# The first gate product of a pass: the input's low half moved to its end, and the wait with it

## The chip, the cores and the metric

The kernel runs on one core of a Trainium2 chip. The metric is the device time of one launch in microseconds, taken as the median of several runs. A second, profiled execution gives the trace from which all rows below are taken.

The engines are named as in the profile: PE is TensorE (matmuls), PEld its weight loads, DVE is VectorE, ACT is ScalarE, POOL is GpSimd, SP is SyncE, which issues the DMAs.

## The reference, cut to what matters

The input is 2 sequences of 1024 tokens with 128 channels. Four blocks follow each other, each with a residual sum and a layer norm without gain ahead of it:

```
x = x + attn_a(layernorm(x))     # a scan over time with a fixed decay per channel
x = x + ffn(layernorm(x))        # 8 experts, all of them for every token
x = x + attn_b(layernorm(x))     # a recurrence with an 8 x 8 state per head
x = x + ffn(layernorm(x))        # the same 8 experts with the same weights
```

The change is in the feed-forward part, which for every expert e is

```
g = einsum('bsh,ehf->ebsf', x, w_gate)
u = einsum('bsh,ehf->ebsf', x, w_up)
h = silu(g) * u
expert_out = einsum('ebsf,efh->ebsh', h, w_down)
out = einsum('ebsh,bse->bsh', expert_out, cw)      # cw: routing weights
```

with 8 experts and 512 hidden channels each.

## The kernel before

**Tiling.** The 2048 tokens are 16 tiles of 128. The feed-forward part goes over them in passes of 4 tiles (512 tokens): passes 0 to 3 are the first feed-forward block, passes 4 to 7 the second. A pass has 32 slots (8 experts by 4 chunks of 128 hidden channels), so there are 256 slots, numbered through: slot 0 opens pass 0, slot 128 pass 4, slot 192 pass 6. A slot g is: the gate product on PE (`gate g`), silu on ACT (`silu g`, line L1049), the up product on PE (`up g`), their product on DVE (`hidden g`, L1662, tile sh_buf), and two halves of the down product on PE (`down g 0`, `down g 1`, w_down by sh_buf). After four slots an expert's sum is scaled on ACT (`weigh`, L1163) and added to x on POOL (`add`, L946).

**Split products.** The normed input of a pass is kept as a high half `z_hi` (a rounded copy, made by ACT at L1029 and counted by the semaphore ln_out) and a low half `z_lo` (what is left, made by DVE at L1673 and counted by z_low). The weights are split alike, into w_hi and w_lo. A gate or up product is three matmuls into one PSUM bank (L1222, through the helper mm): w_hi by z_lo, w_lo by z_hi, w_hi by z_hi. The first gate of a pass waits for z_low ahead of all three.

**What comes ahead of a pass.** For pass q: statistics of x (DVE L1548, L1551; POOL L875, L877), centring and scaling (DVE L1560, L1565, tile normed), four transposes on PE (`ffn_z q`, L1236), the high half on ACT, the low half on DVE (`ffn_low q`), and a full copy zf for the router (`ffn_copy q`, ACT L1036; `route q` on PE).

**What sets the order.** Each engine runs a fixed list. A planner at the head of the file (class Plan, in plain Python, before the kernel is built) makes the lists: every operation has an engine, a duration and a list of what it follows. At each step an engine takes, of the operations that could start within NEAR of the earliest, the one with the highest rank plus a hand-set lead per group (LEAD). The planner also hands out the 8 PSUM banks. So a change in what an operation follows can move operations of every engine. What an engine waits for when it runs is written separately, in the functions that issue the instructions (gate_part, split_product and so on).

**Names used later.** Of attn_a: `mix`, `kv`, `scan`, `r`, `inner` (DVE L1578 to L1608, PE), `mid_T` (PE L1266), `mid_out`, `mid_add`. `restart 0` clears the state tiles for attn_b with four memsets on DVE (L1841 to L1846). Of attn_b's read-out, for pass 3 of it: `y0 3 i` is a product and a reduction on DVE (L1882, L1884), `through` a product on POOL (L936), `y1` a reduction on DVE (L1890); `back_z`, `back_hidden`, `back_out` are on PE, `back_add` (L1916) on DVE.

Of the kernel before, what the change touches and what calls it, by code (L numbers as in the profile page):

```python
# [68 lines left out]
PE_SUM = 1.75  # L69
PE_SUMS = dict(T2=[0, 0, 1, 1, 1, 1, 0, 1, 1, 1, 1, 0, 1, 1, 1, 1], W2=[1, 1, 1, 1, 1, 0, 1, 1, 1, 1, 1, 1, 1, 1, 1, 1])  # L70
SWITCH = 0.08
TABLE_LOAD, HOP, START = 1.28, 0.07, 5.0
CHUNK_TIME = 2.40
WEIGHT = dict(pe=1.60, act=1.10, dve=1.31, pool=1.10, sp=1.02)
# [42 lines left out]
def experts():  # L117

    out = []
    for g in range(SLOTS):  # L120
        q, c = divmod(g, CHUNKS)
        e, f = divmod(g, FC)
        after = (on("pe", "gate", g - 1),) if g else ()
        if c == 0:
            after += (on("dve", "ffn_low", q),)
        if q == 0 and f == 0:
            after += (on("pool", "split", 2 * e), on("pool", "split", 2 * e + 1))
        if g > AHEAD:
            after += (on("dve", "hidden", g - 1 - AHEAD),)
        out.append(pe(("gate", g), 0.7, *after, takes=((("gate", g), on("act", "silu", g)),)))  # L130
        after = (on("act", "silu", g - 1),) if g else ()
        if g >= 2:
            after += (on("dve", "hidden", g - 2),)
        out.append(act(("silu", g), 0.6, on("pe", "gate", g), *after, table="silu"))
        after = (on("pe", "up", g - 1),) if g else ()
        out.append(pe(("up", g), 0.7, on("pe", "gate", g), *after, takes=((("up", g), on("dve", "hidden", g)),)))
        after = (on("dve", "hidden", g - 1),) if g else ()
        if g >= 4:
            after += (on("pe", "down", g - 4, 1),)
        if g == 3:  # L140
            after += (on("pool", "split", 2),)
        out.append(dve(("hidden", g), 0.69, on("act", "silu", g), on("pe", "up", g), *after))
        after = (on("pe", "down", g - 1, 1),) if g else ()
        out.append(pe(("down", g, 0), 0.41, on("dve", "hidden", g), *after, takes=((("y", e), on("act", "weigh", e, 1) if e < PASSES * E - 1 else on("dve", "add_last")),) if f == 0 else ()))
        out.append(pe(("down", g, 1), 0.41, on("pe", "down", g, 0)))
    for e in range(PASSES * E - 1):
        after = (on("pool", "add", e - 1),) if e else ()
        if e % E == 0:
            after += (on("dve", "combine", e // E),)
        out.append(act(("weigh", e, 0), 0.73, on("pe", "down", FC * e + FC - 1, 1), *after))  # L150
        out.append(act(("weigh", e, 1), 0.73, on("act", "weigh", e, 0)))
        out.append(pool(("add", e), 1.26, on("act", "weigh", e, 1), port=True))
    out.append(dve(("add_last",), 1.1, on("pe", "down", SLOTS - 1, 1), on("pool", "add", PASSES * E - 2)))
    return out
# [197 lines left out]
class Plan:  # L352
# [65 lines left out]
    def start(self, k):  # L418
# [15 lines left out]
            begin = max([begin] + [t for t, _ in free[:len(o.takes)]])  # L434
        return begin

    def banks(self):
        out = []
        for name in BANKS:
            freer = self.bank_free[name]  # L440
            if freer is None:
                out.append((0.0, name))
            elif freer in self.end:
                out.append((self.end[freer] + HOP, name))
        return sorted(out)
# [18 lines left out]
    def pick(self, engine):  # L464
        found = []
        for k in self.ready[engine]:
            begin = self.start(k)
            if begin is not None:
                o = self.ops[k]
                if engine == "act" and o.table and o.table != self.table:  # L470
                    found.append((begin + NEAR, begin, k))
                else:
                    found.append((begin, begin, k))
        if not found:
            return None
        near = min(found)[0] + NEAR
        return max((self.ops[k].rank + self.lead(self.ops[k]), -begin, k) for soon, begin, k in found if soon <= near)

    def run(self):
        for k, n in list(self.waiting.items()):  # L480
# [67 lines left out]
def build(nc, a, out):  # L548
    ctx = ExitStack()
    with ctx:  # L550
# [669 lines left out]
        def _(pe):  # L1220
# [99 lines left out]
                if half == 1:  # L1320
                    ins.then_inc(S["y_full" if f == FC - 1 else "d_done"], 1)

            def split_product(bank, lo, hi, q):

                mm(bank, hi, z_lo[:, q % 2, :], stop=False)
                mm(bank, lo, z_hi[:, q % 2, :], start=False, stop=False)
                return mm(bank, hi, z_hi[:, q % 2, :], start=False)

            def sum_rows(bank, product):

# [81 lines left out]
            def gate_part(g):  # L1412
                q, c = divmod(g, CHUNKS)
                e, f = divmod(c, FC)
                cols_f = slice(f * P, (f + 1) * P)
                if c == 0:
                    pe.wait_ge(S["z_low"], q + 1)
                if q == 0 and f == 0:
                    pe.wait_ge(S["w_split"], 2 * e + 2)
                name = BANK["gate", g]  # L1420
                take(name)
                split_product(bank_named[name][:], w_lo[:, e, 0, cols_f], w_hi[:, e, 0, cols_f], q).then_inc(S["g_full"], 1)
                free[name] = (S["silu_done"], g + 1)

            def up_part(g):
# [621 lines left out]
```

## Time and profile before

| | us |
|---|---|
| median of 3 runs | 926.3 (925.91 to 928.23) |
| the profiled execution | 925.21 |
| its span, first to last instruction | 923.2 |
| PE busy in the span | 850.2 (92%) |
| DVE busy | 562.0 (61%) |
| ACT busy | 401.0 (43%) |
| POOL busy | 409.2 (44%) |

The profiled execution is 2.0 us longer than its span and 1.1 us shorter than the median. A busy time is a sum over the span; whether an engine sets the pace of a stretch is read from the stretch, since the program goes through stages in which PE never stops and stages in which PE waits for DVE and POOL.

### The profile page before, as it was taken

The page shows a single profiled execution, that of the slowest core. Times are in us where ns is not written, and L with a number is a line of the kernel's source. Part 1 is how long each engine was busy: PE and PEld are TensorE (multiplying, and loading weights), DVE is VectorE, ACT ScalarE, POOL GpSimd, SP SyncE. Part 2 cuts the span into 40 slices and gives each one's busy share as a digit, 9 for nine tenths or more (in the row PEclk, how much of TensorE's full clock was granted, in tenths as well). Part 3 has the DMA queues.
Part 4 walks back from the last instruction along what each step waited for, and adds up shares of the span by engine and source line. Part 5 has one row for each costly group of instructions (what it writes and reads, how often), then busy time and mean ns, then how long its engine had stood idle before and what let it go on. Part 6 is the DMA issues. An engine that isn't in the chain of part 4 may idle for free.

```text
span 923.2 us, 13835 instructions
## 1 busy us (share of the span) xinstructions
PE 850.2 (92%) x5170; PEld 717.0 (78%) x5170; DVE 562.0 (61%) x927; ACT 401.0 (43%) x874; POOL 409.2 (44%) x287
## 2 busy tenths in 40 slices
PE   3399999989898999999999799799999799999998
PEld 1287987779767888998786487787999678888887
DVE  6669544298819994226698886888112959543222
ACT  5145337653374343334837536134334254544432
POOL 3435311048704876564262674578652624220211
PEclk9699999999999999999999899799999999999999
DMA  9400000011101100012210111111002211000000
GB/s 282 98 1 2 1 1 1 1 46 46 47 1 46 47 24 24 1 47 92 92 46 1 46 47 46 47 46 47 12 1 92 92 46 58 1 2 1 12 1 12
DMA packets 20710, 35.87 MB, mean 39 GB/s; under 512 B 3062, under 2 KB 9636, under 8 KB 20644
## 3 DMA queue, kind: packets, MB, share of 16 engines
q1 hardware_dynamic: 20644, 35.00, 11.5%
q8 instruction: 41, 0.67, 0.3%
q14 instruction: 25, 0.20, 0.1%
HBM read 21.36 MB, written 13.63 MB: 38 GB/s over the span
## 4 chain that ended last, share of the span: by engine, by line
PE 54%; DVE 9%; issue 2%; ACT 1%; POOL 0%; DVEq 0%; ACTq 0%; POOLq 0%
PE bank L1222 53%; DVE states L1882 1%; DVE sh_buf L1662 1%; DVE w_a L1884 1%; DVE backs L1865 1%; DVE scr L1890 1%; DVE state L1786 0%; PE bank L1236 0%; DVE work L1761 0%; DVE state L1794 0%; ACT sh_buf L1049 0%; ACT w_sb L1137 0%; ACT backs L1121 0%; POOL work L888 0%; DVE stats L1548 0%
## 5 line engine op out<-in xcount | busy, mean ns | idle before, releaser
L1662 DVE TENSOR_TENSOR sh_buf<-sh_buf,bank 128x512 f32<-128x512 f32 x256 | 172.8, 684 | 264.2 <-PE bank L1222 225.6
L1222 PEld LDWEIGHTS bank<-w_down,sh_buf 128*128 128x128 f32 x2048 | 274.9, 193 | 47.9 <-DVE sh_buf L1662 24.7
L1222 PE MATMUL bank<-w_down,sh_buf 128*128 128x128 f32 x2048 | 294.8, 281 | 16.2 <-DVE sh_buf L1662 16.2
L1049 ACT ACTIVATE sh_buf<-bank 128x512 f32<-128x512 f32 x256 | 152.3, 598 | 304.7 <-PE bank L1222 227.9
L1222 PE MATMUL bank<-z_lo,w_hi 128*128 128x512 f32 x512 | 234.5, 458 | 0.9 <-DVE z_lo L1673 0.9
L1222 PE MATMUL bank<-z_hi,w_lo 128*128 128x512 f32 x512 | 204.0, 398 | 0.0
L1222 PE MATMUL bank<-z_hi,w_hi 128*128 128x512 f32 x512 | 203.3, 397 | 0.0
L946 POOL TENSOR_TENSOR x<-x,y_weighted 128x512 f32<-128x512 f32 x63 | 88.5, 1405 | 224.7 <-ACT y_weighted L1163 224.7
L1222 PEld LDWEIGHTS bank<-z_hi,w_hi 128*128 128x128 f32 x512 | 96.9, 189 | 23.4
L1222 PEld LDWEIGHTS bank<-z_lo,w_hi 128*128 128x128 f32 x512 | 98.6, 193 | 14.5 <-issue 3.9
L1222 PEld LDWEIGHTS bank<-z_hi,w_lo 128*128 128x128 f32 x512 | 98.6, 193 | 9.0 <-issue 1.2
L926 POOL TENSOR_TENSOR backs<-backs,head_mask 128x512 f32<-128x512 f32 x64 | 70.2, 1101 | 50.5 <-PE bank L1222 45.8
L1163 ACT ACTIVATE y_weighted<-bank,cw 128x128 f32<-128x128 f32 x252 | 72.9, 369 | 24.1 <-PE bank L1222 22.2
L1222 PEld LDWEIGHTS bank<-states,backs 128*128 128x128 f32 x512 | 72.0, 191 | 7.8 <-issue 1.9
L936 POOL TENSOR_TENSOR backs<-backs,w_a 128x1024 f32<-128x1024 f32 x16 | 41.9, 2627 | 62.1 <-DVE w_a L1884 41.1
L1222 PE MATMUL bank<-states,backs 128*128 128x8 f32 x512 | 65.9, 237 | 0.1
L1222 PE MATMUL bank<-work,ident 128*128 128x128 f32 x384 | 51.3, 292 | 9.7 <-DVE work L1761 8.2
L1222 PEld LDWEIGHTS bank<-work,ident 128*128 128x128 f32 x384 | 49.0, 206 | 14.3 <-DVE work L1761 9.6
L1130 ACT ACTIVATE states<-bank 128x16 f32<-128x16 f32 x126 | 23.0, 183 | 70.0 <-PE bank L1222 69.9
L888 POOL TENSOR_TENSOR work<-quad,rkv 128x1024 f32<-128x1024 f32 x16 | 32.3, 2016 | 42.3 <-DVE quad L1737 31.8
L914 POOL TENSOR_TENSOR readout<-state,rkv 128x1024 f32<-128x1024 f32 x16 | 40.5, 2529 | 23.5 <-DVE state L1797 15.1
L906 POOL TENSOR_TENSOR state<-state,work 128x1024 f32<-128x1024 f32 x16 | 43.6, 2724 | 0.9
(206 smaller groups left out, 927.8 us busy)
## 6 DMA issues: line engine op xcount, KB each, us to landing
trans_spill<-state SPq DMA_DIRECT2D x16, 512.0 KB, 2.6
backs<-trans_spill SPq DMA_DIRECT2D x16, 512.0 KB, 3.5
backs<-keep_spill SPq DMA_DIRECT2D x4, 1024.0 KB, 5.5
x<-in_x SPq DMA_DIRECT2D x4, 256.0 KB, 5.2
backs<-in_w_gate SPq DMA_DIRECT2D x4, 256.0 KB, 6.0
backs<-in_w_up SPq DMA_DIRECT2D x4, 256.0 KB, 6.2
keep_spill<-rkv SPq DMA_DIRECT2D x4, 256.0 KB, 2.6
keep_spill<-low SPq DMA_DIRECT2D x4, 256.0 KB, 2.9
```

Of the source, the lines that this page charges most:

```text
L888: pool.tensor_tensor(outer.rearrange("p (h i k) -> p h i k", h=H, i=N), vs[:, i, :].rearrange("p (h i) -> p h i", h=H).unsqueeze(3).broadc ...
L906: pool.tensor_tensor(trans, trans, prod_t, ALU.subtract).then_inc(S["trans_rdy"], 1)
L914: pool.tensor_tensor(readout[:].rearrange("p (h i k) -> p h i k", h=H, i=N), locst.rearrange("p (h i k) -> p h i k", h=H, i=N), over_i(rec ...
L926: pool.tensor_tensor(blocks_d[:, p % RING].rearrange("p c b (h i) -> p (c b) h i", h=H), src.unsqueeze(2).broadcast_to((P, PIECE * B, H, N ...
L936: pool.tensor_tensor(t_ring[t % 2].rearrange("p (h i j) -> p h i j", h=H, i=N), t_ring[t % 2].rearrange("p (h i j) -> p h i j", h=H, i=N), ...
L946: pool.tensor_tensor(flat(x[:, G * j:G * j + G, :]), flat(x[:, G * j:G * j + G, :]), y_weighted[:], ALU.add).then_inc(S["x_added"], 1)
L1049: act.activation(s_buf[:, m % 2, :], bank_of("gate", m)[:], ACT.Silu).then_inc(S["silu_done"], 1)
L1130: act.activation(dst, bank_of("links", u)[:, first:first + B * N].rearrange("p (b k) -> p b k", b=B), ACT.Copy).then_inc(S["link_rdy"], 1)
L1163: ins = act.activation(y_weighted[:, i * P:(i + 1) * P], bank_of("y", eg)[:, i * P:(i + 1) * P], ACT.Identity, scale=cw[:, q % 2, i, e:e + 1])
L1222: return pe.matmul(dst, lhs, rhs, start=start, stop=stop, **kw)
L1662: dve.tensor_tensor(h_buf[:, m % 4, :], s_buf[:, m % 2, :], bank_of("up", m)[:], ALU.mult).then_inc(S["h_done"], 1)
L1865: dve.tensor_tensor(rows_hi(fin_w), rows_hi(locst), dend, ALU.mult).then_inc(S["fin_rdy"], 1)
```

## The change

Three things are changed in the code.

1. In every gate and up product the three matmuls stand in the order w_lo by z_hi, w_hi by z_hi, w_hi by z_lo.
2. The first gate of a pass waits for ln_out (the high half is there) ahead of its first matmul, and for z_low ahead of its third.
3. In the planner, the first gate of a pass follows the high half (`ffn_z q` on ACT) instead of the low half, and the first up product of a pass follows the low half (`ffn_low q`). A term `stick` is added to the priority; its constant STICK is 0.0. LEAD is untouched.

```diff
         if c == 0:
-            after += (on("dve", "ffn_low", q),)
+            after += (on("act", "ffn_z", q),)
...
         after = (on("pe", "up", g - 1),) if g else ()
+        if c == 0:
+            after += (on("dve", "ffn_low", q),)
         out.append(pe(("up", g), 0.7, on("pe", "gate", g), *after, takes=((("up", g), on("dve", "hidden", g)),)))
...
+    def stick(self, k):
+
+        if k[0] != "pe" or not ORDER["pe"]:
+            return 0.0
+        last, kind = ORDER["pe"][-1][0], k[1][0]
+        return STICK if (kind in ("gate", "up") and last in ("gate", "up")) or (kind == last == "down") else 0.0
...
-            def split_product(bank, lo, hi, q):
-
-                mm(bank, hi, z_lo[:, q % 2, :], stop=False)
-                mm(bank, lo, z_hi[:, q % 2, :], start=False, stop=False)
-                return mm(bank, hi, z_hi[:, q % 2, :], start=False)
+            def split_product(bank, lo, hi, q, first=False):
+
+                mm(bank, lo, z_hi[:, q % 2, :], stop=False)
+                mm(bank, hi, z_hi[:, q % 2, :], start=False, stop=False)
+                if first:
+                    pe.wait_ge(S["z_low"], q + 1)
+                return mm(bank, hi, z_lo[:, q % 2, :], start=False)
...
                 if c == 0:
-                    pe.wait_ge(S["z_low"], q + 1)
+                    pe.wait_ge(S["ln_out"], LN["ffn", q] + 1)
...
-                split_product(bank_named[name][:], w_lo[:, e, 0, cols_f], w_hi[:, e, 0, cols_f], q).then_inc(S["g_full"], 1)
+                split_product(bank_named[name][:], w_lo[:, e, 0, cols_f], w_hi[:, e, 0, cols_f], q, c == 0).then_inc(S["g_full"], 1)
```

The planner's lists differ in 40 places on PE, 23 on ACT, 30 on DVE and 4 on POOL, nearly all of them in slots 2 to 17, around slot 35, and in slots 185 to 214. The order at the first gate of passes 0 and 4 is the same as before, the new order inside the product aside. In the changed kernel all line numbers are larger by 10 on PE and by 12 on DVE.

**PE at the head of pass 6.** The row of transposes is `ffn_z 6`. Before, it is followed by down 189, up 191, down 190, then gate 192 (the first gate of pass 6), down 191, gate 193.

```order
L1236 MATMUL bank<-ident,normed 128x128 x4
L1222 MATMUL bank<-w_down,sh_buf 128x128 x4
L1222 MATMUL bank<-z_lo,w_hi 128x512
L1222 MATMUL bank<-z_hi,w_lo 128x512
L1222 MATMUL bank<-z_hi,w_hi 128x512
L1222 MATMUL bank<-w_down,sh_buf 128x128 x4
L1222 MATMUL bank<-z_lo,w_hi 128x512
L1222 MATMUL bank<-z_hi,w_lo 128x512
L1222 MATMUL bank<-z_hi,w_hi 128x512
L1222 MATMUL bank<-w_down,sh_buf 128x128 x4
```

Now up 191 stands ahead of the transposes, and they are followed by down 190 and 191, gate 192, gate 193. The wait for z_low stands ahead of the first z_lo row.

```order
L1232 MATMUL bank<-z_hi,w_lo 128x512
L1232 MATMUL bank<-z_hi,w_hi 128x512
L1232 MATMUL bank<-z_lo,w_hi 128x512
L1246 MATMUL bank<-ident,normed 128x128 x4
L1232 MATMUL bank<-w_down,sh_buf 128x128 x8
L1232 MATMUL bank<-z_hi,w_lo 128x512
L1232 MATMUL bank<-z_hi,w_hi 128x512
L1232 MATMUL bank<-z_lo,w_hi 128x512
L1232 MATMUL bank<-z_hi,w_lo 128x512
```

Down 191 has moved from behind gate 192 to ahead of it, and up 191 from behind the transposes to ahead of them.

**DVE at the same place.** Before, the scaling of the norm is followed by `y0 3 0` (two rows) and then by the low half z_lo; hidden 191 comes behind z_lo.

```order
L1565 TENSOR_TENSOR normed<-normed,rstd 128x512
L1882 TENSOR_TENSOR states<-w_sb,backs 128x1024
L1884 TENSOR_REDUCE w_a<-states 128x128
L1673 TENSOR_TENSOR z_lo<-bank,z_hi 128x512
L1662 TENSOR_TENSOR sh_buf<-sh_buf,bank 128x512
L1882 TENSOR_TENSOR states<-w_sb,backs 128x1024
```

Now hidden 191 stands ahead of `y0 3 0`.

```order
L1577 TENSOR_TENSOR normed<-normed,rstd 128x512
L1674 TENSOR_TENSOR sh_buf<-sh_buf,bank 128x512
L1894 TENSOR_TENSOR states<-w_sb,backs 128x1024
L1896 TENSOR_REDUCE w_a<-states 128x128
L1685 TENSOR_TENSOR z_lo<-bank,z_hi 128x512
L1674 TENSOR_TENSOR sh_buf<-sh_buf,bank 128x512
```

One more operation (hidden 191, which needs up 191 from PE) stands between the norm and the low half.

**PE at slots 15 to 16.** The rows are up 15, gate 16, the first half of down 14, and the transposes `mid_T 2`. Before:

```order
L1222 MATMUL bank<-z_hi,w_hi 128x512
L1222 MATMUL bank<-z_lo,w_hi 128x512
L1222 MATMUL bank<-z_hi,w_lo 128x512
L1222 MATMUL bank<-z_hi,w_hi 128x512
L1222 MATMUL bank<-w_down,sh_buf 128x128 x2
L1266 MATMUL bank<-ident,quad 128x128 x4
```

Now:

```order
L1232 MATMUL bank<-z_lo,w_hi 128x512
L1232 MATMUL bank<-w_down,sh_buf 128x128 x2
L1232 MATMUL bank<-z_hi,w_lo 128x512
L1232 MATMUL bank<-z_hi,w_hi 128x512
L1232 MATMUL bank<-z_lo,w_hi 128x512
L1276 MATMUL bank<-ident,quad 128x128 x4
```

The half of down 14 has moved from behind gate 16 to ahead of it. On DVE, in the same slots, the four memsets of `restart 0` have moved from behind hidden 13 to ahead of hidden 10.

## Rows read from the trace of the kernel before

**Rows 1.** The page, section 1: busy time of each engine.

```profile
PE 850.2 (92%) x5170; PEld 717.0 (78%) x5170; DVE 562.0 (61%) x927; ACT 401.0 (43%) x874; POOL 409.2 (44%) x287
```

**Rows 2.** Busy time by stretch: stretch, its length, then each engine, granted clock, DMA.

```profile
62.00:91.00 29.00, 29.00 (x165) 23.11 (x163) 24.51 (x53) 15.80 (x33) 13.30 (x10) 1.00 0.01 1
493.00:517.00 24.00, 17.87 (x61) 10.41 (x62) 22.63 (x48) 15.22 (x25) 10.05 (x8) 0.91 0.08 23
743.00:820.00 77.00, 76.82 (x450) 63.81 (x450) 49.66 (x92) 37.91 (x73) 21.97 (x17) 1.00 0.10 32
```

**Rows 3.** The page, section 5: the z_lo matmuls; last, the idle time ahead of them.

```profile
L1222 PE MATMUL bank<-z_lo,w_hi 128*128 128x512 f32 x512 | 234.5, 458 | 0.9 <-DVE z_lo L1673 0.9
```

**Rows 4.** Timeline of PE behind gate 192: start, duration, operation.

```profile
763.40 1.05 PE L1222 MATMUL bank<-w_down,sh_buf 128*128 128x128 f32 x8
764.20 0.48 PE L1222 MATMUL bank<-z_lo,w_hi 128*128 128x512 f32 x1
...
764.98 0.40 PE L1222 MATMUL bank<-z_lo,w_hi 128*128 128x512 f32 x1
...
765.68 0.39 PE L1222 MATMUL bank<-z_lo,w_hi 128*128 128x512 f32 x1
```

**Rows 5.** Timeline at gate 0.

```profile
44.67 0.68 DVE L1673 TENSOR_TENSOR z_lo<-bank,z_hi 128x512 fp32r<-128x512 f32 x1
45.57 0.77 PE L1222 MATMUL bank<-z_lo,w_hi 128*128 128x512 f32 x1
```

**Rows 6.** Timeline at gate 128, and PE's next long wait.

```profile
492.12 0.58 ACT L1029 ACTIVATE z_hi<-bank 128x512 fp32r<-128x512 f32 x1
492.73 0.69 DVE L1673 TENSOR_TENSOR z_lo<-bank,z_hi 128x512 fp32r<-128x512 f32 x1 [1.82 <-ACT z_hi L1029]
493.44 0.61 ACT L1144 ACTIVATE states<-ones 32x512 f32<-32x512 f32 x1
493.48 0.50 PE L1222 MATMUL bank<-z_lo,w_hi 128*128 128x512 f32 x1 [0.88 <-DVE z_lo L1673]
...
494.28 1.99 PE L1222 MATMUL bank<-w_a,b_ow 128*128 128x512 f32 x4
...
516.81 1.97 PE L1222 MATMUL bank<-backs,b_w 128*64 128x512 f32 x2 [4.27 <-DVE sh_buf L1662]
```

**Rows 7.** Timeline of PE around gate 192.

```profile
759.48 0.66 PE L1236 MATMUL bank<-ident,normed 128*128 128x128 f32 x4
759.97 1.06 PE L1222 MATMUL bank<-w_down,sh_buf 128*128 128x128 f32 x8
...
761.33 0.40 PE L1222 MATMUL bank<-z_hi,w_hi 128*128 128x512 f32 x1
...
762.59 0.51 PE L1222 MATMUL bank<-z_lo,w_hi 128*128 128x512 f32 x1
```

**Rows 8.** Timeline of DVE around gate 192.

```profile
759.34 1.22 DVE L1882 TENSOR_TENSOR states<-w_sb,backs 128x1024 f32<-128x1024 f32 x1
...
761.85 0.69 DVE L1673 TENSOR_TENSOR z_lo<-bank,z_hi 128x512 fp32r<-128x512 f32 x1
762.46 0.68 DVE L1662 TENSOR_TENSOR sh_buf<-sh_buf,bank 128x512 f32<-128x512 f32 x1
763.05 2.35 DVE L1882 TENSOR_TENSOR states<-w_sb,backs 128x1024 f32<-128x1024 f32 x1
```

**Rows 9.** Timeline of DVE and PE at slots 13 to 16.

```profile
88.68 1.56 DVE L1604 SCALAR_TENSOR_TENSOR work<-rkv,cols,low 128x512 f32<-128x512 f32 x1
...
91.00 1.28 DVE L1662 TENSOR_TENSOR sh_buf<-sh_buf,bank 128x512 f32<-128x512 f32 x2
...
91.74 0.71 PE L1222 MATMUL bank<-w_down,sh_buf 128*128 128x128 f32 x4 [0.72 <-DVE sh_buf L1662]
```

**Rows 10.** The page, section 5: weight loads of one matrix used 8 times running.

```profile
L1222 PEld LDWEIGHTS bank<-work,ident 128*128 128x128 f32 x384 | 49.0, 206 | 14.3 <-DVE work L1761 9.6
L1222 PE MATMUL bank<-work,ident 128*128 128x128 f32 x384 | 51.3, 292 | 9.7 <-DVE work L1761 8.2
```

More of the change, by code:

```diff
@@ L71 @@
 SWITCH = 0.08
+STICK = 0.0
 TABLE_LOAD, HOP, START = 1.28, 0.07, 5.0
@@ L476, in pick @@
         near = min(found)[0] + NEAR
-        return max((self.ops[k].rank + self.lead(self.ops[k]), -begin, k) for soon, begin, k in found if soon <= near)
+        return max((self.ops[k].rank + self.lead(self.ops[k]) + self.stick(k), -begin, k) for soon, begin, k in found if soon <= near)
     def run(self):
```

## The prediction, made before the changed kernel ran

> **What bounds the kernel now.** I read the page first: PE is busy for 850 of 923 us [rows 1]. Then the busy time by stretch, because a mean over the span says nothing about a place. From 743 to 820 us, where pass 6 opens, PE is busy for 76.8 of 77 us: there every microsecond that PE waits is added to the end. From 62 to 91 us PE never stops while DVE fills 24.5 of 29 us, so both are close to the bound. From 493 to 517 us, where pass 4 opens, DVE is busy for 22.6 of 24 us and PE only for 17.9: there DVE sets the pace [rows 2]. Last, how much PE waited for the low half in the whole span: the group of the z_lo matmuls shows 0.9 us, once [rows 3]. That is the most that the late wait can give back directly, and the question is where that 0.9 us lies.
>
> **The new order inside a product costs nothing.** The same 1536 matmuls run. A product directly behind another takes 0.70 us (764.98 to 765.68), so 0.23 per matmul; one behind a down product takes 0.78 (764.20 to 764.98) [rows 4]. The longer first matmul is thus a matter of place, not of z_lo, and will pass to the w_lo row. A down product of two halves and the product behind it take 763.40 to 764.98, 1.58 us, so the two halves add 0.88 to the product's 0.70 wherever they stand [rows 4]. PE work that is only put in another order keeps its sum.
>
> What speaks for a gain is that two matmuls with the same w_hi now follow each other. The trace has such runs: eight matmuls with the identity as weights, 384 in all, and they have 384 weight loads [rows 10]. The load is made each time, beside the matmul ahead of it, and I count nothing. If it fell away and the 27 ns by which the 233 ns of a matmul exceed a load's 206 ns [rows 4, 10] went with it, 512 products would save 14 us. It is the last of the rivals. The Trainium skill ("TensorE: Matmul & The Clock Gate", step-by-step part of the matmul) says that weights can be loaded once and then used by many matmuls; the rows of the identity do not show it.
>
> **Pass 0.** z_lo ends at 45.35, gate 0 starts at 45.57, 0.22 later, while the hop from DVE to PE elsewhere is about 0.05 (762.54 to 762.59) [rows 5, 7, 8]. PE was occupied with transposes and did not wait. Gain 0.
>
> **Pass 4.** Here lies the 0.88 us. The high half is there at 492.70, the low half at 493.42, gate 128 starts at 493.48 [rows 6]. Now it can start at about 492.75, and its third matmul, due at 493.3, waits to 493.47, so the gate ends some 0.5 us sooner. But the next instruction, back_hidden 1 (494.28 before), needs ACT's states tile, which ends at 494.05: PE comes 0.2 us ahead. And PE's next long wait, 4.27 us up to 516.81, is for a hidden product on DVE [rows 6], which stands in a queue that has been full since 492.73 and that neither the gate nor its order enters. So the 0.2 us makes that wait longer and the end no sooner. Gain 0; the bounds are 0 and 0.9.
>
> **Pass 6 loses.** The planner now lets gate 192 follow the high half alone and hangs the low half on up 192. But the engine does what the code says: the wait stands inside gate 192, ahead of its third matmul, and gate 193, which the planner put ahead of up 192 as cover, is queued behind that wait. Arrival on PE: in the old order gate 192 would have started 0.23 + 0.80 us behind the last matmul of up 191 (761.33), at 762.36; it started at 762.59 when z_lo was there, 0.23 late [rows 7, 4]. In the new order down 191 comes first, 0.88 more: gate 192 starts at 763.24 and its third matmul is due at 0.78 - 0.23 = 0.55 later, 763.79. The low half on DVE: hidden 191 now stands ahead of `y0 3 0`. It needs up 191, whose last matmul ended at 761.73; the transposes now come behind it, which puts it 0.49 earlier (759.48 to 759.97), at 761.24 [rows 7]. Hidden 191 starts at 761.29; 0.59 later (762.46 to 763.05) `y0 3 0` starts; 2.51 later (759.34 to 761.85) z_lo starts, and takes 0.69 [rows 8]. z_lo is there at 765.08, PE sees it at 765.13. PE waits 765.13 - 763.79 = 1.34 us, where it waited 0.23 before: **+1.1 us**. All that PE has behind it waits too (gates 193 and 194, ups 192 and 193, route 6), and PE is the bound. The bounds: 0, if DVE comes to `y0 3 0` early enough; 2.2, if its product takes the 2.35 us that one of them took beside POOL's, instead of 1.22 [rows 8].
>
> The other moves from slot 185 to 214 (back_hidden, back_out, back_z 3, ffn_z 7 each one or two tasks later) find their inputs ready by my walk through both queues; `y0 3 1` comes about 4.5 us later, since hidden 192 now stands ahead of it and needs up 192.
>
> **Slots 2 to 17.** The half of down 14 needs hidden 14 and waited for it: DVE 91.00 plus 0.69, PE at 91.74 after 0.72 us of idle time, with gate 16 already done [rows 9]. DVE's queue up to hidden 14 holds the same work as before (the four memsets of restart 0 only come earlier), and it is nearly without a gap, so hidden 14 stays at about 91.6. But gate 16 (0.70 us) now stands behind the half of down 14, and comes that much later. From this I take 0.2 for gaps that DVE loses: **+0.5 us**. PE waits in two places for it, before down 12 (hidden 12 is pushed back by the memsets) and before down 14. Until 147 us every wait of DVE is for PE, so the delay is handed on. Bounds: 0.8, gate 16 whole; -0.4, if L1604, which took 1.56 us at 88.68, falls beside no POOL work any more and saves 0.8.
>
> **Slot 35 and around 300 us:** a front norm 0.4 us later and two tasks swapped, all with a margin behind them. 0, with 0.3 either way.
>
> **The sum.** The profiled execution took 925.2; 925.2 + 1.1 + 0.5 = 926.8. It lies 1.1 below the median of the runs, so against the median the forecast is 926.3 + 1.6 = **927.9 us**. A measurement of this kernel can tell about 0.3% (2.8 us) from no change, so this is "the same" with a loss inside.
>
> **Rivals.**
> - **Nothing moves.** `y0 3 0` starts before PE needs the low half, and the waits of the early slots only change places: 926.3, within 925.3 to 927.0. For it: the sums at both places are differences of tenths between queues. Against it: in pass 6 a hidden product that needs PE is put ahead of z_lo, and 2.5 us of DVE work lies between.
> - **Slower: DVE becomes the bound of pass 6.** PE's slot is about 2.3 us; DVE's share of it is 0.69 plus a `y0` of 2.5 in every other slot. If the later `y0` meet POOL's products, each takes 1.13 more (2.35 against 1.22 [rows 8]). Three of them make 3.4 us, of which the 1.4 us or so that hidden products run ahead of their down products swallow a part: 2.0 more, on top of 1.6, 929.9. It decides from the second slow one on. Against it: at 743 to 820 us DVE is busy for only 49.7 of 77 us [rows 2].
> - **Faster: pass 4 hands its gain on.** From 493 to 517 us the granted clock is 0.91 on average [rows 2], so part of it ran at 1.2 GHz. If an idle time less kept PE at 2.4 GHz for the W2 sum that follows 516.81, DVE's chain behind it would gain some 2 to 4 us: 923. Against it: the 4.27 us wait ahead of it stays and even grows.
> - **Weights are not loaded twice:** 926.3 - 14 = 912, against 384 loads for 384 matmuls [rows 10].
>
> **How the numbers follow.** Forecast (927.0 to 929.1) 0.50; nothing moves 0.28; slower by DVE or by a stretch at the low clock behind the new wait 0.14; faster by pass 4 0.07; loads 0.01. Forecast and "nothing moves" lie within 0.3% (923.5 to 929.1). So faster 0.08, same 0.78, slower 0.14. The range reaches from 924.4, which takes in the lower bounds of slots 2 to 17 and of pass 4 and the spread of the runs, to 930.2, which takes in the DVE case: 924.4 to 930.2.
>
> **What would show it.** In the changed profile: the first w_lo row of gate 128 at about 0.7 us after the high half starts to be read, and the long wait before front_hidden 3 still over 4 us; the z_lo matmuls with an idle time of about 1.3 us by z_lo at gate 192 and some 0.2 at gate 128; `y0` rows between hidden 191 and z_lo on DVE; an idle time of about 0.9 before the half of down 14, with gate 16 behind it; the w_lo matmuls now with the larger mean, near 458 ns, and z_lo's near 397. The sum is wrong if gate 192's third matmul does not wait, if the early waits are below 0.5 us, or if the stretches at the lower clock change in number or length: one of them moved is worth as much as all my terms together.

## The result, and the profile after

The changed kernel took **928.27 us** (median of 12 runs, 926.5 to 929.85) against 926.96 us (12 runs, 924.91 to 928.51) of the kernel before beside it: ratio **1.0023**, 95% interval 1.0013 to 1.0032. By this ratio it is 2.1 us more: inside the 0.3% that the prediction counts as the same, and with an interval above 1. The ratio is not the quotient of the two medians, which lie only 1.31 us apart; the size of the loss is known no better than that from the times. In a second series it was 1.0021 (1.0007 to 1.0035). The profiled execution took 928.20 us, its span 926.3 us at a mean clock of 0.967; before, 925.21 and 923.2 us at 0.972. In the second series its span was 924.2 at 0.973. The two traces of one kernel thus differ by 2.1 us, as much as the change costs, and the difference of two whole spans proves nothing here. What can be compared are stretches between two fixed tasks, which agree between traces to some hundredths of a microsecond where the granted clock is alike. One profiled execution, that of the experiment code_only, took 1687 us and is left out everywhere.

The busy time by stretch after the change answers to [rows 2] (stretch, its length, then each engine, granted clock, DMA):

```profile
62.00:91.00 29.00, 28.11 (x161) 22.57 (x161) 24.97 (x53) 15.82 (x33) 11.91 (x9) 1.00 0.00 1
493.00:517.00 24.00, 16.97 (x64) 9.14 (x62) 22.10 (x47) 15.86 (x26) 9.25 (x8) 0.94 0.07 23
743.00:820.00 77.00, 75.31 (x438) 61.71 (x437) 47.19 (x86) 37.04 (x72) 21.72 (x15) 1.00 0.10 31
```

PE never stopped in the first stretch and was busy for 76.8 us in the last; now it stops for 0.9 and for 1.7 us. The page's groups of the products, with the idle time ahead of them, answer to [rows 3]:

```profile
L1232 PE MATMUL bank<-z_hi,w_lo 128*128 128x512 f32 x512 | 234.8, 459 | 0.2 <-ACT z_hi L1039 0.2
L1232 PE MATMUL bank<-z_lo,w_hi 128*128 128x512 f32 x512 | 204.2, 399 | 1.1 <-DVE z_lo L1685 1.1
L1232 PE MATMUL bank<-z_hi,w_hi 128*128 128x512 f32 x512 | 204.9, 400 | 0.0
```

The mean of 459 ns has passed from z_lo to w_lo, and the idle time by z_lo is 1.1 us, where it was 0.9: the change was to take a wait for z_lo away and has more of it. It only lies elsewhere. PE at gate 192 (start, duration, operation, idle time before):

```profile
762.82 0.66 PE L1246 MATMUL bank<-ident,normed 128*128 128x128 f32 x4
763.31 1.95 PE L1232 MATMUL bank<-w_down,sh_buf 128*128 128x128 f32 x16
765.01 0.48 PE L1232 MATMUL bank<-z_hi,w_lo 128*128 128x512 f32 x1
765.33 0.39 PE L1232 MATMUL bank<-z_hi,w_hi 128*128 128x512 f32 x1
766.86 0.50 PE L1232 MATMUL bank<-z_lo,w_hi 128*128 128x512 f32 x1 [1.14 <-DVE z_lo L1685]
767.21 0.39 PE L1232 MATMUL bank<-z_hi,w_lo 128*128 128x512 f32 x1
```

And DVE ahead of it:

```profile
757.02 0.69 DVE L1928 TENSOR_TENSOR x<-x,bank 128x512 f32<-128x512 f32 x1 [2.83 <-PE bank L1232]
...
761.41 0.69 DVE L1674 TENSOR_TENSOR sh_buf<-sh_buf,bank 128x512 f32<-128x512 f32 x1 [1.06 <-ACT sh_buf L1059]
762.02 0.74 DVE L1577 TENSOR_TENSOR normed<-normed,rstd 128x512 f32<-128x512 f32 x1
763.01 0.69 DVE L1674 TENSOR_TENSOR sh_buf<-sh_buf,bank 128x512 f32<-128x512 f32 x1 [0.25 <-issue]
763.61 1.22 DVE L1894 TENSOR_TENSOR states<-w_sb,backs 128x1024 f32<-128x1024 f32 x1
764.87 1.22 DVE L1896 TENSOR_REDUCE w_a<-states 128x128 f32<-128x1024 f32 x1
766.12 0.69 DVE L1685 TENSOR_TENSOR z_lo<-bank,z_hi 128x512 fp32r<-128x512 f32 x1
768.86 0.69 DVE L1674 TENSOR_TENSOR sh_buf<-sh_buf,bank 128x512 f32<-128x512 f32 x1 [2.05 <-PE bank L1232]
```

Hidden 191 (763.01), the two instructions of `y0 3 0`, then z_lo: DVE reaches it at 766.12 and the third matmul waits. The rows of pass 4 answer to [rows 6]:

```profile
493.54 0.50 PE L1232 MATMUL bank<-z_hi,w_lo 128*128 128x512 f32 x1 [0.15 <-ACT z_hi L1039]
493.88 0.40 PE L1232 MATMUL bank<-z_hi,w_hi 128*128 128x512 f32 x1
494.26 0.50 PE L1232 MATMUL bank<-z_lo,w_hi 128*128 128x512 f32 x1
494.60 1.99 PE L1232 MATMUL bank<-w_a,b_ow 128*128 128x512 f32 x4
...
517.63 1.97 PE L1232 MATMUL bank<-backs,b_w 128*64 128x512 f32 x2 [6.08 <-DVE sh_buf L1674]
```

Here the change does what it says: the wait at the gate is 0.15 us instead of 0.88. And PE's next long wait is 6.08 us instead of 4.27, so none of it arrives.

**Stretches between tasks.** All traces of this study in one table: microseconds from the start of the first task's first matmul to that of the second's. The kernels are explained with the experiments below. "Lists" says whose order of the work they run; a number is that of the tasks put elsewhere in it.

```
                          lists      gate 8-  gate 40- gate 127-  gate 133- gate 187- gate 195- gate 205-
                                     mid_T 2  gate 48  fr_hid 3 5 gate 170  gate 195  gate 205  gate 220
before                    before      27.52    30.38    36.10     144.16     24.63     22.94     41.39
code_again                before      27.55    30.38    36.11     144.15     24.53     22.94     43.00
extra                     before      27.54    30.38    36.09     144.11     25.53     22.93     41.39
out_late                  before+1    27.54    30.37    36.10     144.14     26.19     22.94     41.39
after                     after       27.77    30.54    36.12     144.79     25.84     22.94     41.61
after_again               after       27.77    30.51    36.10     144.04     25.85     22.94     41.60
plan_only                 after       27.75    30.52    36.09     144.82     26.32     22.94     41.61
low_first                 after+1     27.76    30.51    36.10     144.69     24.44     24.19     41.61
low_y_late                after+2     27.78    30.56    36.11     144.03     24.43     24.18     42.97
out_early                 after+4     27.77    30.54    36.10     144.71     25.12     22.94     41.61
early_back                after+2     29.31    30.53    36.09     144.77     27.40     22.94     41.60
```

From gate 220 to the last down product every trace has 84.99 us. The loss of the changed kernel is in four places: +1.21 us where pass 6 opens, +0.25 in slots 8 to 17, +0.22 between gates 205 and 220, +0.16 between gates 40 and 48: 1.84 us in all, between the 1.3 us of the medians and the 2.1 us of the ratio.

The two small ones are waits too short for the profile to name. Between gates 205 and 220 it is the transposes of pass 7 in the changed kernel:

```profile
822.39 0.69 DVE L1577 TENSOR_TENSOR normed<-normed,rstd 128x512 f32<-128x512 f32 x1 [0.65 <-POOL rstd L887]
822.55 0.60 PE L1232 MATMUL bank<-w_down,sh_buf 128*128 128x128 f32 x4
823.14 0.66 PE L1246 MATMUL bank<-ident,normed 128*128 128x128 f32 x4
```

The norm is ready at 823.08 and the transposes start at 823.14, 0.59 us behind the half of a down product; before, the same step took 0.45 us. Their norm is late because `back_add 3`, which it follows, starts 23.77 us behind gate 205 instead of 21.92: `back_out 3` has come later on PE. Between gates 40 and 48 the first products that read the front's hidden layer (`tokA 0 0`) start at 164.73, 0.05 us after ACT ended that layer (164.68); before, ACT was 0.45 us ahead (163.73 and 164.18).

### The profile page after: what moved, and what is told of

Its sections match the earlier page's. It is cut to its first block, busy times and chain, and to the rows that moved or that the text cites. A ratio compares the mean times of both kernels' runs of the same rounds, so it can differ in the third digit from the quotient of the medians.

```text
span 926.3 us, 13835 instructions
## 1 busy us (share of the span) xinstructions
PE 851.7 (92%) x5170; PEld 716.9 (77%) x5170; DVE 559.4 (60%) x927; ACT 401.9 (43%) x874; POOL 408.3 (44%) x287
## 4 chain that ended last, share of the span: by engine, by line
PE 50%; DVE 10%; issue 3%; POOL 2%; ACT 1%; DVEq 0%; POOLq 0%; ACTq 0%
PE bank L1232 50%; DVE states L1894 1%; DVE sh_buf L1674 1%; DVE w_a L1896 1%; DVE backs L1877 1%; POOL state L916 1%; DVE scr L1902 0%; DVE state L1798 0%; POOL work L906 0%; POOL work L898 0%; DVE work L1773 0%; DVE state L1809 0%; DVE state L1806 0%; DVE quad L1764 0%; POOL readout L924 0%
## 5 line engine op out<-in xcount | busy, mean ns | idle before, releaser
L1232 PEld LDWEIGHTS bank<-w_down,sh_buf 128*128 128x128 f32 x2048 | 274.3, 192 | 49.3 <-DVE sh_buf L1674 24.4
L1232 PE MATMUL bank<-z_hi,w_lo 128*128 128x512 f32 x512 | 234.8, 459 | 0.2 <-ACT z_hi L1039 0.2
L1232 PE MATMUL bank<-z_lo,w_hi 128*128 128x512 f32 x512 | 204.2, 399 | 1.1 <-DVE z_lo L1685 1.1
L1232 PEld LDWEIGHTS bank<-z_hi,w_hi 128*128 128x128 f32 x512 | 98.8, 193 | 9.1 <-issue 1.2
```

Source lines behind the costliest of these rows:

```text
L1232: return pe.matmul(dst, lhs, rhs, start=start, stop=stop, **kw)
```

## Experiments

Each was timed in five rounds beside the kernel before; ratios are to it, with 95% intervals. Nothing is left out of the computation in any of them. In the diffs `move(engine, task, target)` takes a task out of the finished list of an engine and puts it ahead of the target, with `False` behind it.

### code_only and code_again: the new engine code under the old lists

Against the changed kernel, in the planner's rules for gate and up:

```
         if c == 0:
-            after += (on("act", "ffn_z", q),)
+            after += (on("dve", "ffn_low", q),)
...
-        if c == 0:
-            after += (on("dve", "ffn_low", q),)
```

> The new order inside the products and the late wait for z_low, with the planner's rules of before, so every engine's list of operations is that of before. Theory (the loss is in the planner's lists): no loss. Gate 128 starts 0.7 us sooner and the end does not move; at gate 192 the 0.23 us of waiting goes. From gate 187 to gate 195 the trace shows 24.4 us (24.63 before). Time: that of before, -0.2 to 0 us. Rival (the new product order or the wait inside the gate costs by itself): 1 us or more slower than before. Second rival (pass 4's 0.88 us is worth something): 0.5 to 0.9 us faster.

> The changed engine code (the low half's product last, with its own wait) under the lists of the kernel before; the same text as code_only, for a profile that can be read. Theory (the code is free, its lists are what costs): within 0.1% of before; in the profile gate 8 to mid_T 2 takes 27.5 us as before (27.76 with the new lists), gate 187 to gate 195 takes 24.63 or, with the 0.23 us of waiting at gate 192 gone, 24.4 (25.8 with the new lists), gate 195 to 205 22.94, gate 205 to 220 41.39; gate 128 starts 0.7 us earlier and the wait ahead of front_hidden 3 5 is near 5 us instead of 4.27, so gate 127 to front_hidden 3 5 stays at 36.1. Rival (the late wait itself or the longer first matmul costs): the 1.2 us of pass 6 are there with the old lists too, 0.13% slower.

Measured: code_only 925.51 us, ratio 0.9990 (0.9976 to 1.0005). The same text ran again as code_again: 926.52 us, 1.0003 (0.9991 to 1.0015), span 924.2. The page of code_again:

```profile
L1230 PE MATMUL bank<-z_hi,w_lo 128*128 128x512 f32 x512 | 234.4, 458 | 0.2 <-ACT z_hi L1037 0.2
L1230 PE MATMUL bank<-z_hi,w_hi 128*128 128x512 f32 x512 | 203.9, 398 | 0.0
L1230 PE MATMUL bank<-z_lo,w_hi 128*128 128x512 f32 x512 | 203.6, 398 | 0.0
```

PE never waits for z_lo any more: both of the waits that there were, 0.88 at gate 128 and 0.23 at gate 192, are gone. Pass 6 gains 0.10 (24.53 against 24.63), pass 4 nothing. So the code itself costs nothing, and of the 0.9 us that the wait for z_lo showed, the end gets some 0.1. The expected 24.4 was 24.53.

### plan_only: the new lists under the old engine code

Against the kernel before, in the same rules:

```
         if c == 0:
-            after += (on("dve", "ffn_low", q),)
+            after += (on("act", "ffn_z", q),)
...
+        if c == 0:
+            after += (on("dve", "ffn_low", q),)
```

> The new lists of the planner with the engine code of before: z_lo first in every product, the wait ahead of all three matmuls. Theory: the loss stays and grows by the two matmuls that may no longer run ahead of the wait at gate 192, 0.55 us: PE waits about 1.8 us there, gate 187 to gate 195 takes 26.4 us (25.84 in the changed kernel, 24.63 before). Time: 0.5 us above the changed kernel, 2 to 3 above before. Rival (the cost is in the code): the time of before.

Measured: 929.50 us, 1.0030 (1.0015 to 1.0045). Gate 187 to gate 195 takes 26.32 us, and the three smaller losses have their full size (27.75, 30.52 and 41.61 us in the table). All of the loss is here, without the change's code, and the code takes back 0.5 of it (25.84): with the wait ahead of the whole product, its first two matmuls stand behind z_lo too.

### low_first: the low half ahead of `y0 3 0`

```
+move("dve", ("ffn_low", 6), ("y0", 3, 0))
```

> The changed kernel with one operation moved on DVE: the low half of pass 6 stands ahead of y0 3 0 instead of behind it. Theory (the 2.5 us of y0 ahead of z_lo make PE wait): the low half is there before PE needs it, the wait of 1.14 us at gate 192 is gone, gate 187 to gate 195 takes 24.6 us instead of 25.84, and the time is 1.2 us below the changed kernel. Rival (PE would have lost the same time behind it, on hidden products or banks): the wait goes and others take its place, time as the changed kernel.

Measured: 929.43 us, 1.0023 (1.0010 to 1.0035): nothing gained. At gate 192 the expected 1.2 us are there: gate 187 to gate 195 fell from 25.84 to 24.44 us. But from gate 195 to gate 205 it takes 24.19 us instead of 22.94. The one wait that PE's timeline shows from 762 to 795 us:

```profile
773.60 1.16 PE L1240 MATMUL bank<-w_down,sh_buf 128*128 128x128 f32 x8 [0.90 <-DVE sh_buf L1682]
```

It is down 193, which needs hidden 193, and DVE ahead of that:

```profile
768.31 0.69 DVE L1682 TENSOR_TENSOR sh_buf<-sh_buf,bank 128x512 f32<-128x512 f32 x1 [0.36 <-ACT sh_buf L1067]
768.92 2.65 DVE L1902 TENSOR_TENSOR states<-w_sb,backs 128x1024 f32<-128x1024 f32 x1
771.60 1.22 DVE L1904 TENSOR_REDUCE w_a<-states 128x128 f32<-128x1024 f32 x1
772.85 0.69 DVE L1682 TENSOR_TENSOR sh_buf<-sh_buf,bank 128x512 f32<-128x512 f32 x1
```

Hidden 192, `y0 3 1`, hidden 193. The first instruction of `y0 3 1` takes 2.65 us instead of 1.22, and a POOL product runs beside it:

```profile
768.09 2.39 POOL L954 TENSOR_TENSOR backs<-backs,w_a 128x1024 f32<-128x1024 f32 x1 [5.14 <-issue]
```

In the changed kernel `y0 3 1` starts at 769.46, behind the POOL product, and takes 1.22. Here, what is taken from one wait is paid in the next.

### low_y_late: `y0 3 1` out of the way as well

```
+move("dve", ("ffn_low", 6), ("y0", 3, 0))
+move("dve", ("y0", 3, 1), ("hidden", 193), False)
```

> low_first (the low half of pass 6 ahead of y0 3 0) with y0 3 1 moved behind hidden 193 as well. In low_first the 1.2 us gained at gate 192 went again between gates 195 and 205 (24.19 us instead of 22.94), where the half of down 193 waited for a hidden product behind y0 3 1. Theory (that place in DVE's queue is what costs): gate 195 to 205 falls to 22.9 to 23.3 us, gate 187 to 195 stays at 24.4, and the time is 0.8 to 1.2 us below the changed kernel's, 0.10 to 0.14% over before. Rival (DVE has no room there, so any order of it hands the 1.2 us to another wait): gate 187 to 205 stays at 48.6 and the time at 0.2% over before.

Measured: 927.91 us, 1.0008 (0.9996 to 1.0019). The theory's place is clean, down 193 no longer waits, yet gate 195 to gate 205 takes 24.18 us as in low_first. The longest wait stands three slots further on, at down 196, and shorter ones that no row names stand around it:

```profile
777.73 1.16 PE L1241 MATMUL bank<-w_down,sh_buf 128*128 128x128 f32 x8 [0.56 <-DVE sh_buf L1683]
```

The rival holds for the stretch: wherever the two `y0` stand, about 1.2 us reach PE by gate 205 (gate 187 to 205: 48.78 in the changed kernel, 48.63 and 48.61 in these two, 47.57 before). That the median is nevertheless below low_first's does not come from this stretch. The timed runs differ in clock: the mean granted clock of its 12 runs is 0.9715, that of low_first's 12 is 0.9659. That this is the whole difference is not shown.

### out_late: one move in the kernel before

If neither of two other orders of DVE's queue in pass 6 helps, its work may arrive too late as a whole. PE's timeline ahead of pass 6 shows how it could. `back_out 2`, the 3.3 us of W2 products that feed the residual, stands ahead of gate 189 in the old list; in the new one it stands behind gate 189, up 188 and half of down 187, 1.84 us of PE work later. DVE's `back_add 2` (757.02 in the changed kernel, released by PE), the norm of pass 6, z and both `y0` hang on it.

code_only with one line more:

```
+move("pe", ("back_out", 2), ("down", 187, 0), False)
```

> code_only (the changed engine code under the lists of before) with one task moved: back_out 2 on PE, the 3.3 us that feed the residual of pass 6, stands behind gate 189, up 188 and the first half of down 187, as it does in the changed kernel, instead of ahead of gate 189. Theory (what costs in pass 6 is that its chain, back_add, norm, z, low half, starts 1.84 us of PE work later, and DVE's two y0 with it): gate 187 to gate 195 grows from 24.5 us to 25.6 to 26.0, z_lo's matmul at gate 192 waits some 1 to 1.5 us for DVE, the time is 0.1 to 0.15% over before. Rival (the places of hidden 191 and y0 3 0 on DVE are the cause, as forecast): gate 187 to 195 stays within 0.3 of 24.5 and the time within 0.03% of code_only.

Measured: 928.51 us, 1.0019 (1.0006 to 1.0033). This single move in the old lists costs more than the new lists do: gate 187 to gate 195 is 26.19 us, against 24.53 in code_again without it and 25.84 in the changed kernel: 1.66 us, somewhat more than expected. The waits are not at z_lo, though:

```profile
761.46 1.16 PE L1238 MATMUL bank<-w_down,sh_buf 128*128 128x128 f32 x8 [0.68 <-DVE sh_buf L1680]
763.88 0.66 PE L1252 MATMUL bank<-ident,normed 128*128 128x128 f32 x4 [0.55 <-DVE normed L1583]
```

PE waits for a hidden product behind `back_add 2` and for the norm itself, since this list has the transposes early. The new lists put them behind up 191 and so turned these two waits into one, at z_lo.

### out_early: the head of the chain put back in the changed kernel

```
+move("pe", ("back_out", 2), ("gate", 189))
+move("pe", ("up", 190), ("down", 188, 0))
+move("dve", ("hidden", 188), ("ffn_centre", 6), False)
+move("dve", ("y0", 3, 0), ("hidden", 191))
```

> The changed kernel with the head of pass 6's chain put back: on PE back_out 2 ahead of gate 189 and up 190 ahead of down 188, on DVE hidden 188 behind ffn_centre 6 and y0 3 0 ahead of hidden 191; gate 192, the transposes and the low half stay where the change put them. Theory (the chain's start is the cause): norm 6 and y0 3 0 start 1.1 to 1.9 us earlier, z_lo is there before gate 192's third matmul is due, gate 187 to 195 falls from 25.8 to 24.4 to 24.9, gate 195 to 205 stays below 23.3, the time is about 0.1% below the changed kernel's, so 0.10 to 0.13% over before. Rival (DVE hands the 1.2 us on whatever stands first, as in low_first and low_y_late): gate 187 to 205 stays at 48.6 to 48.8.

Measured: 927.29 us, 1.0015 (1.0002 to 1.0027). Gate 187 to gate 195 falls to 25.12 us and gate 195 to gate 205 stays at 22.94: gate 187 to 205 is 48.07, so 0.71 of the 1.21 us are back and are **not** paid later. It missed the expected 24.4 to 24.9 by one wait, which `y0 3 0` ahead of hidden 191 makes:

```profile
764.48 1.16 PE L1243 MATMUL bank<-w_down,sh_buf 128*128 128x128 f32 x8 [0.54 <-DVE sh_buf L1685]
```

z_lo is there in time; no row of gate 192 waits. In the ratios the step from 1.0023 to 1.0015 lies inside the intervals; the stretches carry the verdict.

One thing this experiment does not separate. It puts back the start of the chain and, with `y0 3 0` ahead of hidden 191, also the order that the prediction named as the cause. The trace of the changed kernel says that the early start alone would not have brought z_lo sooner: there DVE stood idle for 0.25 us ahead of hidden 191 (763.01), which needs up 191 from PE. The old lists with hidden 191 alone ahead of `y0 3 0` were not run.

### extra: what 0.9 us on PE are worth at the two gates

The kernel before, ahead of the first gate's product:

```
+                if g in (4 * CHUNKS, 6 * CHUNKS):
+                for _ in range(4):
+                    mm(bank_named[name][:], w_hi[:, e, 0, cols_f], z_hi[:, q % 2, :])
```

> The kernel before, with four more matmuls of w_hi and z_hi (0.93 us) in front of the product at gate 128 and at gate 192; their result is overwritten. It measures where 0.9 us on PE count. Theory (pass 4 is paced by DVE, pass 6 by PE): of gate 128's 0.93 us nothing arrives, gate 127 to front_hidden 3 5 stays at 36.1 and the wait of 4.27 ahead of it falls to about 3.3; at gate 192 all 0.93 arrives, gate 187 to 195 grows from 24.63 to 25.5 and the end by 0.9 us: 0.10% slower. Rival (PE counts alike at both places): both grow by 0.93, 0.20% slower.

Measured in the trace: gate 127 to front_hidden 3 5 is 36.09 us, as in every other kernel. Of pass 4's 0.93 us nothing arrives. Gate 187 to gate 195 is 25.53, 0.90 more, and the last down product starts 0.9 later relative to gate 187: of pass 6's all arrives. The theory's sizes are right. Its wait of "about 3.3" was not: it is 4.87 us, since this trace has no low clock at 503 us (granted clock 0.99 from 493 to 517, against 0.91), so PE arrived earlier in spite of the added work, and still gained nothing. The four matmuls themselves:

```profile
762.91 1.20 PE L1222 MATMUL bank<-z_hi,w_hi 128*128 128x512 f32 x4
763.95 0.39 PE L1222 MATMUL bank<-z_lo,w_hi 128*128 128x512 f32 x1
```

The time does not show it: 926.09 us, 0.9995 (0.9985 to 1.0005), where the trace would give 1.0010. The clocks of the timed runs say where to look. The mean granted clock of its 12 runs is 0.9725, that of the 29 runs of before beside it 0.9699, and among those 29 the spans are 923.5 us at a clock of 0.972 and 925.9 us at 0.968. Where the two kernels have runs at the same clock, extra's span (one run at each) is longer than the mean of before's each time: 926.7 against 925.5 us at 0.970, 924.9 against 924.3 at 0.971, 924.7 against 923.5 at 0.972. Why extra ran at the higher clock more often is open. Two medians of this kernel can't be told apart to a microsecond unless their clocks are alike.

### early_back: the early slots

```
+move("dve", ("restart", 0), ("inner", 3))
+move("pe", ("gate", 16), ("down", 14, 0))
```

> The changed kernel with the two moves of the early slots undone: restart 0 back behind its place before inner 3 on DVE, gate 16 back ahead of the half of down 14 on PE. Theory: gate 8 to mid_T 2 falls from 27.76 to 27.5 us, gate 187 to 195 stays at 25.8, and the time is 0.25 us (0.03%) below the changed kernel's, so 0.17 to 0.2% over before. Rival (more of the loss comes from the early slots than the interval shows): 0.1% or less over before.

Measured: 931.52 us, 1.0048 (1.0032 to 1.0064); both theories missed. Gate 8 to mid_T 2 takes 29.31 us, 1.5 more than in the changed kernel. The half of down 14 now waits for hidden 14 like this:

```profile
94.07 0.71 PE L1241 MATMUL bank<-w_down,sh_buf 128*128 128x128 f32 x4 [1.76 <-DVE sh_buf L1683]
```

In the old lists the memsets follow a z_lo at 85.53; in the new ones this z_lo is at 88.63, three microseconds later, and the memsets put behind it push hidden 14. It is no undoing of one part: two tasks of a list were put back into a list in which their neighbours had moved. Of the rest, 1.56 us lie where pass 6 opens (27.40 us against 25.84): this trace has a granted clock of 0.50 from 759.5 to 762.9 us, inside that stretch. The size of the early slots comes from code_again instead, 27.55 against 27.77.

### after_again: the changed kernel once more

> The changed kernel once more, as a control on the same chip and for a second trace. Theory: 1.2 to 1.7 us slower than before; gate 187 to gate 195 takes 25.8 us again and gate 8 to the transposes mid_T 2 27.8 us again (27.52 before). The stretch at 1.2 GHz at 640 us, which the first trace of it shows and before's does not, may be absent: then the profiled span is about 0.8 us shorter.

Measured: 928.61 us, 1.0021 (1.0007 to 1.0035). Its stretches in the table repeat those of the first trace to 0.03 us, except one: gate 133 to gate 170 takes 144.04 instead of 144.79. The first row is that of the first trace, the second that of the second at the same time (columns as in the busy time by stretch; the last but two is the granted clock):

```profile
640.40:643.80 3.40, 3.40 (x9) 2.67 (x9) 3.33 (x4) 3.40 (x5) 1.81 (x2) 0.50 0.02 5
```

```profile
640.40:643.80 3.40, 2.87 (x14) 1.78 (x12) 2.97 (x4) 2.85 (x5) 3.11 (x3) 1.00 0.06 22
```

A granted clock of 0.50 (1.2 GHz) for 3.4 us costs 0.75 us there. It is in five of the seven traces with the new lists or lists near them, and in none of the four with the old ones; eleven traces are too few to say whether the lists have a part in it.

## Why the prediction was right, and where it was not

The forecast was 927.9 us and "the same, with a loss inside"; it came to 928.27. That the number is so near is in part luck. The forecast stood on a median of 926.3 us from three runs, and 12 runs of the same kernel gave 926.96: the step was forecast as 1.6 us and is 1.3 by the medians, 2.1 by the ratio and 1.84 by the stretches. And inside the 1.84 one term came to half its size, while 0.38 us came from places that were put at nothing. Step by step:

- **New order inside a product: 0.** Right. code_again holds it, and the means passed from row to row as said (459 and 399 ns against 458 and 397).
- **Loads: no gain.** Right. The page of after has 512 loads for each of the three kinds of product, and z_hi,w_hi and z_lo,w_hi follow each other with the same weights:

```profile
L1232 PEld LDWEIGHTS bank<-z_lo,w_hi 128*128 128x128 f32 x512 | 97.5, 190 | 25.4 <-DVE z_lo L1685 2.0
L1232 PEld LDWEIGHTS bank<-z_hi,w_hi 128*128 128x128 f32 x512 | 98.8, 193 | 9.1 <-issue 1.2
```

- **Pass 4: 0.** Right, with its reason. The freed 0.7 us made the wait for DVE longer; even 0.93 us of added work came to nothing.
- **Pass 6: +1.1.** It measured +1.21. Shifted by the 1.69 us by which this trace is late at gate 188, hidden 191 ran at 761.32 (forecast 761.29), z_lo started at 764.43 (764.39), the third matmul started 1.30 us after it was due (1.34). The missing 0.1 is the matmul behind a wait: from it to the next are 0.35 us, not 0.23.
- **But its cause went only half the way.** The prediction named hidden 191 ahead of `y0 3 0` as what makes z_lo late, and for the wait at gate 192 that is what the trace shows. low_first puts z_lo ahead of `y0 3 0`, and the loss comes back 8 us later, so there is more to it. What the prediction said of the other moves (back_hidden, back_out and others, each one or two tasks later) is that they "find their inputs ready". That is true and is the step that misled: back_out's inputs are ready, but whoever needs its output, DVE's whole chain of pass 6, gets it 1.84 us of PE work later. I asked of each moved task whether it must wait, and not who waits for it. Out_late shows that this move alone costs 1.66 us; taking it back together with three others, `y0 3 0` among them, brings 0.71. So two things act here, the late chain and the order on DVE, and the loss of 1.21 us is less than the late chain cost alone; only the late chain was run by itself. The sum was right all the same because hidden 191 had to wait for up 191 in any case, which the prediction had in its walk.
- **The DVE rival** (`y0` meeting POOL, 2.0 more) did not come in the changed kernel: three of its four `y0` products took 1.22 us and the last 1.50. It did come in low_first, with 2.65 us, and there it hands on what was gained.
- **Slots 2 to 17: +0.5.** Half of it. PE waits 0.89 us, ahead of down 12 alone:

```profile
85.92 0.71 PE L1232 MATMUL bank<-w_down,sh_buf 128*128 128x128 f32 x4 [0.89 <-DVE sh_buf L1674]
...
91.52 0.71 PE L1232 MATMUL bank<-w_down,sh_buf 128*128 128x128 f32 x4
91.99 0.48 PE L1232 MATMUL bank<-z_hi,w_lo 128*128 128x512 f32 x1
```

  Two waits were forecast, ahead of down 12 and of down 14, where there had been one of 0.72 [rows 9]. The first came, the second did not: hidden 14 started at 90.78 instead of 91.00 (0.46 earlier, counted from gate 8, at which this trace is 0.24 us late), since L1604 (now L1616) took 0.74 us instead of 1.56: before, it started at 88.68 beside a POOL addition that had run since 88.41; now the addition starts at 89.50, after L1616 has (89.29), and it is the addition that is longer (1.68 us instead of 1.28). That was in the bounds as a gain of up to 0.8, and I took too little of it. Net +0.25.
- **Put at nothing:** +0.16 from gate 40 to 48 and +0.22 from gate 205 to 220, in every kernel with the new lists and in none with the old. The first lies behind the changes at slot 35, for which "0, with 0.3 either way" was given "with a margin behind": the 0.45 us that ACT was ahead were all but used up. The second is again a moved `back_out` whose inputs are ready and whose output is late, this time by 1.85 us, of which PE pays 0.22. They make up, by luck, for what the slots did not cost: 1.1 + 0.5 was forecast, 1.84 measured.
- **The clock.** The prediction said that a moved stretch at the low clock weighs as much as its terms. One came, near 640 us, and one near 503 us went (the granted clock from 493 to 517 us rose from 0.91 to 0.94); the first costs 0.75 us and the second nothing, since DVE sets the pace there. The first trace of the changed kernel also stayed at the low clock 3.4 us longer at the program's start, which reaches gate 8 at 65.0 us instead of 64.3 in the second trace. How often the 0.75 comes on top in the timed runs no trace tells; their mean granted clock is 0.970 in the 12 runs of the changed kernel and in 85 runs of the kernel before alike.

## What to carry to other kernels

When a planner is given a looser rule, look at the whole list that it makes, not at the wait that the rule removes: the wait for z_lo was 0.9 us and 0.1 of it was worth having, while the list that came with it moved a 3.3 us block that a chain of the other engine starts from, put one more task ahead of z_lo, and lost 1.2. For each moved task ask two questions: do its inputs exist yet, and who waits for its output. And where two engines are both nearly full, moving a wait out of one place shows nothing until the stretch behind it, up to where the engines have slack again, has been read as well.

## What the runs showed of the hardware

A granted clock of 0.50 for 3.4 us does not cost the same everywhere. Where PE is never idle it cost 1.6 us, near the 1.7 us that half the clock over 3.4 us would take (code_again, gate 205 to 220, 43.00 against 41.39; low_y_late has one there too and pays 1.36):

```profile
813.80:817.20 3.40, 3.40 (x14) 3.02 (x13) 2.69 (x11) 0.60 (x1) 1.40 (x2) 0.54 0.01 2
```

Ahead of gate 187 it cost 0.8 (gate 170 to 187: 63.2 us with such a stretch at 731 us, 62.4 to 62.5 in the three traces without), since PE waits for DVE behind it: out_early's trace has a wait of 1.91 us there. In pass 4 it cost nothing. And code_again, which has none at 731, has one at 814 instead. Where they fall differs between two traces of one kernel, and moves a single trace by as much as the change does.

The DVE product of `y0` (128x1024) takes 1.22 us with no POOL work beside it and up to 2.65 us in the rows above: a difference larger than any of the waits in question. What its length depends on can be read off. The eleven traces have 47 places where it starts while a POOL product of `through`, of the same size, is running. In all of them it ends 1.08 to 1.10 us after POOL's does, whether it started 0.06 or 2.25 us behind POOL's start (POOL's end and DVE's: 764.32 and 765.40 in before, 770.48 and 771.57 in low_first), and it takes up to 3.39 us (out_late, at 728.46). In these places DVE gained next to nothing by starting while POOL was at work.
